# Three orders inside the step of a pipelined two-layer FFN kernel: x1, the low parts and the gates on VectorE, the roundings and sigmoids on ScalarE

## The reference, cut to what matters

```python
# layer 0: grouped convolution of 9 taps along the 512, plus ctx and bias
y0 = conv(x) + ctx(cond)[:, :, None] + bias
x1 = x + ffn0(y0)
# layer 1: one 32x32 mixing matrix per sample, from a small MLP on cond
y1 = einsum('boi,bih->boh', agg_w, x1) + agg_b[:, :, None]
out = x1 + ffn1(y1)

def ffn(y):                         # y: tokens x 512
    logits = y @ W_router.T         # 8 of them
    w = softmax of the top two      # 0 for the other six
    h = y @ A.T                     # 8 experts x rank 16
    return y @ W_base.T + b_base + 2 * (h * w) @ B
```

## Time and profile before

| what | value |
|---|---|
| median of three runs | 419.71 us |
| the profiled execution, its own time | 419.07 us |
| its span, first to last instruction | 417.3 us |
| TensorE, matmuls | 393.8 us busy (94%), 2789 instructions |
| TensorE, weight loads (beside the matmuls) | 375.2 us (90%) |
| VectorE | 282.4 us (68%) |
| ScalarE | 210.6 us (50%) |
| GpSimd | 226.7 us (54%) |
| memory traffic | 31.04 MB, 74 GB/s on average |

### The profile page before, as it was taken

How to read it: one execution, slowest core, us unless ns; L and a number is a source line. 1 busy time by engine, 2 the same in 40 slices (tenths; PEclk the granted TensorE clock), 3 DMA queues, 4 the chain that set the end, 5 groups by cost and what they waited for, 6 DMA issues and landing times.

```text
span 417.3 us, 9113 instructions
## 1 busy us (share of the span) xinstructions
PE 393.8 (94%) x2789; PEld 375.2 (90%) x2789; DVE 282.4 (68%) x982; ACT 210.6 (50%) x529; POOL 226.7 (54%) x199
## 2 busy tenths in 40 slices
PE   7979999999999999999999999999999999999995
PEld 6668999999999999999999999999999999999985
DVE  3878766766676676676667667667666766766764
ACT  5756544555454455454455555445554544554441
POOL 3577556645446655445665544566454466554460
PEclk9999999999999999999999999999999999999999
DMA  8851222121222212122221212221112222121101
GB/s 262 295 113 45 77 77 77 53 51 52 74 76 76 76 27 74 50 76 76 76 60 41 64 62 76 76 76 50 51 52 74 76 76 74 29 74 50 53 26 52
DMA packets 19677, 31.04 MB, mean 74 GB/s; under 512 B 5904, under 2 KB 5936, under 8 KB 19664
## 3 DMA queue, kind: packets, MB, share of 16 engines
q1 hardware_dynamic: 19664, 30.89, 24.3%
HBM read 21.97 MB, written 8.91 MB: 74 GB/s over the span
## 4 chain that ended last, share of the span: by engine, by line
PE 73%; DVE 9%; issue 8%; ACT 6%; DMA 1%; DVEq 1%; POOL 0%; SPq 0%; ACTq 0%
PE ps_out L331 34%; PE ps_out L343 11%; PE ps_conv L299 10%; PE ps_out L363 6%; DVE x L767 5%; ACT yT L476 5%; PE ps_mix L377 5%; PE ps_t L311 3%; PE ps_mix L380 2%; DVE yT L625 2%; DMA wa_raw<-in_wa 1%; PE ps_t L350 1%; DVE wb L625 1%; PE ps_out L350 1%; DVEq L691 0%
## 5 line engine op out<-in xcount | busy, mean ns | idle before, releaser
L331 PE MATMUL ps_out<-wa,yT 128*128 128x392 f32 x768 | 156.7, 351 | 14.1 <-DVE x L767 12.8
L331 PEld LDWEIGHTS ps_out<-wa,yT 128*128 128x128 f32 x768 | 130.2, 188 | 26.5 <-ACT yT L476 18.0
L879 POOL TENSOR_TENSOR x_part<-x,x_part 128x512 fp32r<-128x512 f32 x31 | 40.1, 1294 | 139.8 <-ACT x_part L476 139.8
L343 PE MATMUL ps_out<-wb,yT 128*128 128x256 f32 x768 | 104.1, 285 | 0.4 <-DVE wb L625 0.4
L343 PEld LDWEIGHTS ps_out<-wb,yT 128*128 128x128 f32 x768 | 95.8, 189 | 0.6 <-issue 0.6
L476 ACT ACTIVATE yT<-ps_t 64x256 fp32r<-64x256 f32 x128 | 48.4, 378 | 29.3 <-PE ps_t L311 26.9
L363 PE MATMUL ps_out<-lb_w,hwT 128*128 128x256 f32 x384 | 59.4, 289 | 1.4 <-ACT hwT L476 0.7
L513 ACT ACTIVATE wts<-top 128x1 f32<-128x1 f32 x128 | 30.8, 287 | 57.7 <-DVE top L716 57.0
L625 DVE TENSOR_TENSOR yT<-ps_t,yT 64x256 fp32r<-64x256 f32 x128 | 54.1, 422 | 5.4 <-ACT yT L476 0.3
L892 POOL TENSOR_TENSOR x1b<-x,base_bias 128x512 f32<-128x512 f32 x31 | 41.0, 1323 | 25.0 <-DVE res L752 25.0
L363 PEld LDWEIGHTS ps_out<-lb_w,hwT 128*128 128x128 f32 x384 | 49.8, 189 | 2.5 <-ACT hwT L476 1.2
(11 more groups left out here) (91 smaller groups left out, 496.7 us busy)
## 6 DMA issues: line engine op xcount, KB each, us to landing
x_raw<-in_x_phase SPq DMA_DIRECT2D x32, 260.0 KB, 2.7
x_tok<-in_x_tok SPq DMA_DIRECT2D x32, 256.0 KB, 2.6
out<-res SPq DMA_DIRECT2D x31, 256.0 KB, 2.1
wa_raw<-in_wa SPq DMA_DIRECT2D x2, 784.0 KB, 7.4
wb_raw<-in_wb SPq DMA_DIRECT2D x2, 512.0 KB, 8.4
lb_raw<-in_lb SPq DMA_DIRECT2D x2, 256.0 KB, 5.5
bias<-in_bias SPq DMA_DIRECT2D x2, 256.0 KB, 5.6
scratch<-mix_nat SPq DMA_DIRECT2D x1, 512.0 KB, 2.8
```

The lines of the kernel that those rows point to most:

```text
L331: last = mm(out_banks(y, t)[:, 0, 0:AR + DH], yT[y][dp][:, k, :], wa[y][:, wp, k, :], start=(n == 0 and k == 0), stop=(n == len(SPLITS) - ...
L343: last = mm(out_banks(y, t)[:, 1, OUT], yT[y][dp][:, k, :], wb[y][:, wp, k, :], start=(n == 0 and k == 0), stop=False, skip_group_check=True)
L879: g.tensor_tensor(x1_part[LO][:, :], x1[:, :], x1_part[HI][:, :].bitcast(F32), ALU.subtract).then_inc(s["x1l"], 1)
```

## The change

Two `step` functions are put in another order. No instruction is added or taken away, no semaphore and no wait is changed, and TensorE, GpSimd and SyncE keep their streams. The prologue and the tail keep theirs too, so steps 1 to 30 differ.

```diff
 # ScalarE, step(t)
                 turned_hw(0, t)
                 turned0(t + 1, 0)
-                weigh(1, t - 1)
                 turned0(t + 1, 1)
                 split_x1(t)
+                weigh(1, t - 1)
                 pass_bias(t)
 # VectorE, step(t)
                 turned_hw(0, t)
                 choose(1, t - 1)
+                middle(t)
                 turned0(t + 1, 0)
-                middle(t)
+                turned0(t + 1, 1)
                 gate(1, t - 1)
-                turned0(t + 1, 1)
                 if isinstance(t, int) and t == 1:
                     low_lb(1)
```

## The result

Four runs of the changed kernel gave 397.82, 399.21, 399.58 and 400.40 us, a median of **399.39 us** against 419.64 for the kernel before in four runs. The ratio is 0.951, 95% interval 0.948 to 0.953. The forecast was 399.0, the range 397.0 to 405.5. The profile is of the run of 400.40, with a span of 398.6.

The account below looks back on a forecast made before the run. TensorE, 94% busy at full clock, was taken to bound the kernel, stalling for x1 each turn. Saving 0.59 for the start and 0.10 for the restart, times 30, gives 20.7 us: 419.71 - 20.7 = 399.0 us, range 397.0 to 405.5.

Parts of the forecast that it names:

- 0.59 + 0.13: TensorE's loss per turn at layer 0's first product: late start 0.59 us, slower twelve matmuls 0.13; ceiling 0.72.
- the idle row: TensorE's listed wait for x1, 0.43 us a turn, 12.8 in all; rival that only this returns: 406.9 us, chance 0.06.
- the restart: Slow start of TensorE's stalled first product, its weight load paid in the open; 0.10 us a turn counted as saved.
- the term of 0.03: Remainder of the first product's 0.13 us beside the restart's 0.10; counted as no gain, the ninth matmul's margin staying thin.
- "about 21" us: Total saving if a stalled TensorE product also pays its weight load in the open, against 12.8 by idle time alone.
- The upper end: Saving taken as 0.69 us a turn, 20.7 in all, near the ceiling of 0.72 a turn, 21.6 in all.
- The lower end: Fast end of the main case's own range, 397.4 us: ceiling saving of 21.6 and 0.5 for the lower runs.
- the low part of x1: GpSimd's low part of x1 ends at 223.72, ahead of the mixing product's need, covered by 0.3 us; no cost.
- The cover of `hw`: Gates last on VectorE make layer 1's `hw` ready later, about 224.05, wanted at 225.1: covered by 1 us, no cost.
- A stop at the ninth matmul: Rival: x1 or low quarters 0.3 us late leave a smaller stop, 0.2 us lost a turn, 405.0 us; chance 0.17.
- The slower side: Rival: late `b_product(0)` or `xb` delays all low quarters; equality at x1 0.75 us late, for example 430 us; chance 0.04.
- The signs: Expected profile: x1 wait gone, TensorE near 99% busy, x1 0.1 us behind `choose`, low quarters ending 2.4 us after x1's start.

Follow-up runs that it names:

- VectorE's part alone: The changed kernel with ScalarE's step in its old order, VectorE's in the new: 408.24 us, 0.970 of the kernel before.
- x1 moved alone: The kernel before with only VectorE's x1 instruction moved ahead of sample 0's low quarters: 419.58 us, 0.997 of the kernel before.
- ScalarE's part alone: The changed kernel with VectorE's step in its old order, ScalarE's in the new: 456.64 us, 1.085 of the kernel before.
- The pads: The changed kernel with an unused VectorE memset of 128x128, 128x512 or 128x1024 between x1 and the low quarters: 400.40, 410.61 and 427.25 us.
- the pads of 512 and 1024: The changed kernel with an unused VectorE memset of 128x512 or 128x1024 between x1 and the low quarters: 410.61 and 427.25 us.
- the sigmoids first: The changed kernel with ScalarE's sigmoids ahead of the rounding of x1, both behind the high quarters: 402.25 us, 0.957 of the kernel before.
- the prologue variant: The changed kernel with GpSimd's low part of the mixing matrices ahead of its low part of x1 in the prologue: 397.97 and 397.99 us.
- the repeated changed kernel: The changed kernel unaltered, run again beside a later group of runs: 398.18 us, 0.948 of the kernel before.
- the pad of 128: The changed kernel with an unused VectorE memset of 128x128 between x1 and the low quarters: 400.40 us, one run.

## Why the prediction was right, point by point

**The size of the stall.** The step that carried the forecast was to take a turn's loss from starts, 0.59 + 0.13, and not from the idle row, 0.43. The changed kernel has exactly the undisturbed distances, 1.43 and 2.15. The idle row alone would have given 406.9 us.

Of the 0.29 us beyond the idle row, the prediction has the restart as the reason, and that covers 0.11 only. The second matmul of the stalled product starts 0.28 us behind the first, at 222.91, where it is 0.18 in the changed kernel (214.50); the other ten distances differ by 0.03 together, the term of 0.03. In the stalled turn the weight load starts with its matmul:

```profile
222.63 2.12 PEld L331 LDWEIGHTS ps_out<-wa,yT 128*128 128x128 f32 x12 [0.63 <-ACT yT L476]
```

In the changed kernel it starts 0.12 ahead, at 214.20, so that a weight load is paid in the open after a stall is borne out. The remaining 0.16 has nothing to do with it: the idle row counts from the modelled end of the second product, 222.20, and an undisturbed product starts 0.16 before that, at 222.04. So the "about 21" us that the prediction gives beside it doesn't follow from the weight load; the sum of 0.59 and 0.10, taken from starts, is what holds.

**The upper end.** I took 0.69 and left 0.03, for a ninth matmul still held. It wasn't: the low quarters end at 215.51, the ninth is due at 214.32 + 1.43 = 215.75, so 0.24 us remain, where I had 0.18. x1 starts at 213.13, 0.07 behind the modelled end of the product at 213.06, not 0.13. The restart and the hold both went, which is 0.03 x 30 = 0.9 us more than forecast. The lower end has a small slip: 419.71 - 21.6 - 0.5 is 397.6, not 397.4; nothing hangs on it.

**VectorE.** x1 and four low quarters took 2.38 us as in the prologue. The gates ended at 216.25, 3.12 us behind the start of x1, where the working has 3.14, and the idle time ahead of the next routing is 0.42, forecast 0.4.

**ScalarE.** Four high quarters took 1.59. That they must move too was shown by VectorE's part alone: 0.34 us a turn, about half of the gain. That the low quarters must also come ahead of the gates is shown by x1 moved alone beside VectorE's part alone, which differ in nothing else: 12.22 and 11.88. That the sigmoids can't stand behind x1's rounding while low quarters stand behind the gates, ScalarE's part alone shows. The change is not a sum of independent parts: x1 alone gives 0.05, VectorE's new order 0.39, and ScalarE's adds 0.34 to it; by itself ScalarE's costs 1.21.

**The covers.** I costed the low part of x1 at nothing with 0.3 us in hand. In the timeline it ends 0.47 ahead of the mixing product, less 0.18 for its weight load; delaying it by 0.36 cost 0.12 a turn. The cover of `hw`, 1 us, was not tested by itself.

**The rivals.** A stop at the ninth matmul was kept at 0.17 and priced at 0.2 us for 0.3 us of lateness. The pads show the real curve: 0.49 costs 0.41, so 0.3 would cost about 0.2 by that line. The slower side needed x1 0.75 us late; the pads, which delay only the low quarters, put equality with the kernel before (12.27) between delays of 0.49 and 1.02, by a straight line at about 0.8. That `b_product(0)` or `xb` could come late by so much was not tested.

**The signs.** The wait for x1 went, x1 stands 0.03 us behind `choose`, the low quarters end 2.38 us behind its start, and the rounding 0.02 behind the fourth high quarter. One sign missed: TensorE's busy share is 97% and not near 99%. Between tiles 3 and 31 it is 100%; the rest is the prologue and the tail.

**The median.** The profiled run came out at 400.40 and not at 398.4. It lost 1.29 us ahead of all changed steps and 0.81 up to tile 2, where the clock fell; the prediction had nothing for either. That the median lies within 0.4 us of the forecast is in part luck: the saving by medians was 20.25 us in the first group of runs and 420.02 - 398.18 = 21.84 in the second. What the runs bear out is the 0.72 us of a turn.

## What to carry to other kernels

A wait list names the operand that came last; before moving it, work out when each of the others would be there, since x1 alone was worth 0.05 us of 0.72. Measure a stall by the distance between starts against an undisturbed group of the same shape: the idle time in the profile, 0.43 us, left out 40% of it, 0.16 by the modelled end and 0.11 by the restart. An engine with little to do can still be the one to reorder in an in-order stream, and its order has to be moved together with that of the engines that read from it.

## What the runs showed of the hardware that I had not expected

**The granted clock fell for some microseconds in the prologue, in some executions.** In the profiled run of the changed kernel, windows of 2 us show (TensorE busy, weight loads busy, VectorE, ScalarE, GpSimd, then granted clock as a share of 2.4 GHz, DMA share, GB/s):

```profile
28.00:30.00 2.00, 0.67 (x4) 0.34 (x2) 1.93 (x6) 0.13 (x1) 2.00 (x2) 1.00 0.21 81
30.00:32.00 2.00, 1.96 (x12) 1.99 (x13) 1.02 (x6) 1.06 (x4) 1.19 (x1) 0.72 0.00 0
32.00:34.00 2.00, 2.00 (x12) 2.00 (x11) 0.80 (x2) 1.97 (x6) 0.54 (x1) 0.50 0.46 133
34.00:36.00 2.00, 2.00 (x16) 2.00 (x16) 0.88 (x2) 1.76 (x3) 2.00 (x3) 0.93 0.00 0
```

TensorE was idle from 28.7 to 30.0, then worked, and the clock was at its lower level, 1.2 GHz, for about 3 us while it did. The stretch from tile 1's to tile 2's first product took 14.58 us instead of 13.23: 1.35 us. VectorE's part alone has the same idle stretch and the clock stayed full, so the idle stretch is not enough to bring it about. The kernel before has that stretch too, 1.36 us, at a full clock. In the pads of 512 and 1024, with x1 moved alone and with the sigmoids first it fell between 12 and 24 us instead, ahead of all that differs between these kernels; in the profiled runs of the kernel before, of the two parts alone and of the prologue variant no such fall is seen. That chance alone sets the place isn't borne out either: the repeated changed kernel and the pad of 128 had it at 28 to 36 us again. Its cause stays open.

It is not the only source of the spread between runs of one kernel, and perhaps not the main one. The two profiled runs of the prologue variant, 397.45 and 399.39 us, both have a full clock there; tile 1's first product starts at 24.56 in one and at 26.57 in the other, and that is all of the difference. The profiled run of the changed kernel was the slowest of its group both times, so its fall of the clock need not be in the others.

**A GpSimd instruction took four times its usual length beside VectorE work.** The low part of the mixing matrices took 2.00 us in the prologue beside a VectorE subtraction with two SBUF operands (128x1568, 1.96 us), and 0.46 in the loop:

```profile
27.66 1.96 DVE L625 TENSOR_TENSOR wa<-wa_raw,wa 128x1568 fp32r<-128x1568 f32 x1
27.94 2.00 POOL L869 TENSOR_TENSOR mix_part<-mix,mix_part 128x128 fp32r<-128x128 f32 x1
```

It ends at 29.94, some 0.3 us behind the end of VectorE's. The Trainium skill, SBUF — State Buffer, section Who interferes with whom, says that a VectorE instruction with two SBUF inputs and a GpSimd one that reads SBUF exclude each other for the whole of an instruction, the second waiting for the first. The trace agrees here: 1.5 us are added, and in the variant where GpSimd had finished this part before VectorE's began it took 0.46. There GpSimd's next instruction was under way when VectorE's began, and VectorE's took 2.57 us instead of 1.96.
